# Identity products on TensorE, a weight wait split in two, and another order of the first loads in a graph layer with experts

## What is computed

```python
def graph_layer(h, adj, W_proj, b_proj, W_gcn, b_gcn):      # h = layernorm(x)
    filt = tanh(adj * adj) * (adj > 0)
    vals, idx = top_k(filt, 350)                            # per row
    new_adj = zeros_like(filt).at[rows, idx].set(vals)      # kept entries alone
    h2 = tanh(h @ W_proj + b_proj)
    return relu(new_adj @ (h2 @ W_gcn) + b_gcn)

def experts(x, Wg, bg, W1, b1, W2, b2):                     # x = layernorm(x)
    scores, idx = top_k(x @ Wg.T + bg, 2)
    probs = softmax(scores)
    return sum over e of combine[e] * (relu(x @ W1[e].T + b1[e]) @ W2[e].T + b2[e])

x = x + graph_layer(layernorm(x), adj, ...)
x = x + experts(layernorm(x), ...)
```

## Time and profile before

| | |
|---|---|
| three runs | 468.95, 470.61 and 470.99 us; median 470.61 |
| the profiled execution | 468.27 us, its span 466.5 us |
| mean granted clock of TensorE | 0.965 of the full 2.4 GHz |
| HBM | 77.9 MB read, 12.7 MB written, 194 GB/s over the span |

### The profile page before, as it was taken

One profiled execution on the slowest core, in us unless ns is written; L12 is line 12 of the kernel. 1 busy time (PEld: TensorE's weight loads), 2 busy tenths in 40 slices (PEclk: granted clock), 3 DMA queues, 4 the chain that ended last, 5 costly groups with the idle time before them and its releaser, 6 DMA issues.

```text
span 466.5 us, 8103 instructions
## 1 busy us (share of the span) xinstructions
PE 396.0 (85%) x2456; PEld 242.2 (52%) x2456; DVE 366.1 (78%) x959; ACT 339.5 (73%) x345; POOL 205.6 (44%) x266
## 2 busy tenths in 40 slices
PE   0999989999788789999998979969798989999600
PEld 0455534444334244455454434436698989989500
DVE  5999978998999999985999999999976444444235
ACT  2789998889979778859999769973565656666400
POOL 3049961000004501800740638821777777777700
PEclk9999999999999979999999999989999999999955
DMA  7839976778357666873875757854745655631069
GB/s 227 328 120 373 351 290 231 265 279 306 136 193 257 227 225 228 274 260 145 302 253 211 259 191 279 288 137 75 109 91 161 106 114 107 92 79 51 23 218 326
DMA packets 57074, 95.42 MB, mean 205 GB/s; under 512 B 36740, under 2 KB 44088, under 8 KB 48832
## 3 DMA queue, kind: packets, MB, share of 16 engines
q1 hardware_dynamic: 45840, 79.80, 52.7%
q0 software_dynamic: 6048, 12.72, 9.0%
q10 hardware_dynamic: 5136, 2.30, 1.7%
HBM read 77.90 MB, written 12.67 MB: 194 GB/s over the span
## 4 chain that ended last, share of the span: by engine, by line
DVE 50%; PE 23%; issue 12%; DMA 5%; ACT 4%; POOL 4%; ACTq 1%; SPq 1%; DVEq 0%; POOLq 0%
DVE marks L856 17%; PE bank L1350 5%; ACT tbuf L1091 3%; PE bank L1438 3%; PE bank L1458 3%; PE bank L1459 3%; PE bank L1460 2%; PE bank L1440 2%; PE bank L1439 2%; POOL expert_rows L631 2%; DMA tbuf<-expert_rows 2%; DVE rowbf L707 2%; PE bank L1297 2%; DVE tbuf L1012 2%; DVE nrm L780 1%
## 5 line engine op out<-in xcount | busy, mean ns | idle before, releaser
L1350 PE MATMUL bank<-tbuf,g_sb 128*128 128x512 f32 x512 | 236.0, 609 | 2.5 <-ACT tbuf L1095 1.6
L617 POOL DMA_INDIRECT routed_rows<-aug,slots x64 | 87.9, 1373 | 153.3 <-DVE base L834 135.6
L1350 PEld LDWEIGHTS bank<-tbuf,g_sb 128*128 128x128 f32 x512 | 95.6, 195 | 111.8 <-issue 104.7
L856 DVE SCALAR_TENSOR_TENSOR marks<-abuf,marks 128x2048 bf16<-128x2048 int32 x56 | 129.4, 2312 | 1.1
L1091 ACT ACTIVATE tbuf<-abuf 128x2048 f32<-128x2048 f32 x64 | 121.5, 1898 | 4.8 <-PE bank L1350 2.6
L1095 ACT ACTIVATE tbuf<-tbuf 128x2048 f32<-128x2048 f32 x64 | 122.3, 1911 | 2.0
L631 POOL DMA_INDIRECT expert_rows<-abuf,xmeta x78 | 76.8, 985 | 23.8 <-issue 22.0
L1012 DVE SCALAR_TENSOR_TENSOR tbuf<-bank,tbuf 128x512 f16<-128x512 f32 x78 | 50.2, 685 | 45.8 <-ACT tbuf L1198 43.0
L1458 PE MATMUL bank<-w2h,tbuf 128*128 x312 | 54.4, 219 | 2.4 <-DVE tbuf L1012 2.4
L1460 PE MATMUL bank<-w2h,tbuf 128*128 x312 | 54.3, 219 | 0.0
L1459 PE MATMUL bank<-w2l,tbuf 128*128 x312 | 54.3, 219 | 0.0
(11 more groups left out here) (216 smaller groups left out, 434.3 us busy)
## 6 DMA issues: line engine op xcount, KB each, us to landing
abuf<-in_adj_tiles SPq DMA_DIRECT2D x64, 1024.0 KB, 5.5
wstage<-in_w POOLq DMA_DIRECT2D x16, 256.0 KB, 6.5
tbuf<-expert_rows SPq DMA_DIRECT2D x8, 512.0 KB, 7.3
out<-xres ACTq DMA_DIRECT2D x8, 256.0 KB, 6.3
expert_rows<-abuf,xmeta POOLq DMA_INDIRECT x78, 2.3
routed_rows<-pad SPq DMA_DIRECT2D x9, 130.0 KB
routed_rows<-aug,slots POOLq DMA_INDIRECT x64
abuf<-routed_rows SPq DMA_TRANSPOSE x39
```

The source lines that it names most:

```text
L617: pool.indirect_dma_start(xs, bass.IndirectOffsetOnAxis(ap=slots[:, i % 2, k * SUB + cc:k * SUB + cc + 1], axis=0), aug[:, i % 2, k, cc, : ...
L856: dve.scalar_tensor_tensor(mark, bits_in, 1.0, mark, ALU.min, ALU.add).then_inc(s_raw, 1)
L1350: last = pe.matmul(ps_feat[ib % 2][:, :], g_sb[:, c, :], tbuf[:, buf, cc, :], start=(c == 0), stop=(c == C - 1))
```

## The change

- `load_x(1)` moves from ahead of chunk 0's load to behind it, and `load_x(2)` from behind chunk 0 to behind chunk 1.
- ScalarE issues W_proj first, with a semaphore of its own, `s_wp`. TensorE waits for it alone ahead of `project(0)`, and for the other three ahead of `gcn(0)`.
- ScalarE squares chunk 0 ahead of copying out group 0.
- TensorE multiplies the identity with itself 26 times (`WARM`) into bank 3 once the identity is there. The results are never read.

```diff
@@ -49,6 +49,7 @@
     NTA = NT
+    WARM = 26
     PW = 512
@@ -249,6 +250,7 @@
     s_w = sem("s_w")
+    s_wp = sem("s_wp")
@@ -406,14 +408,13 @@
             load_x(0)
-            load_x(1)
             for n in range(NCH):
                 if n >= NBUF:
                     sp.wait_ge(s_sq, n - NBUF + 1)
                     sp.wait_ge(s_raw, n - NBUF + 1)
                 sp.dma_start(abuf[:, n % NBUF, :, :], adj_tiles[n // NK, n % NK, :, :, :]).then_inc(s_a[n % NBUF], 16)
-                if n == 0:
-                    load_x(2)
+                if n < 2:
+                    load_x(n + 1)
@@ -1077,8 +1078,8 @@
+            act.dma_start(wp_sb[:, :], w_proj).then_inc(s_wp, 16)
             act.dma_start(bp_sb[:, :], b_proj.rearrange("(p o) -> p o", o=1)).then_inc(s_w, 16)
-            act.dma_start(wp_sb[:, :], w_proj).then_inc(s_w, 16)
             act.dma_start(wg_sb[:, :], w_gcn).then_inc(s_w, 16)
@@ -1111,9 +1112,9 @@
+            square_chunk(0)
             turned_out(0)
-            square_chunk(0)
-            act.wait_ge(s_w, 64)
+            act.wait_ge(s_w, 48)
             projected_out(0)
@@ -1246,6 +1247,9 @@
             pe.wait_ge(s_ident, 1)
 
+            for i in range(WARM):
+                pe.matmul(bank[3][:, 0:P], ident[:, :], ident[:, :], start=True, stop=True)
+
@@ -1269,8 +1273,9 @@
             turn_group(0)
-            pe.wait_ge(s_w, 64)
+            pe.wait_ge(s_wp, 16)
             project(0)
+            pe.wait_ge(s_w, 48)
             gcn(0)
```

## The result

In one comparison of 8 runs each, before's median was 469.81 us and the changed kernel's 472.81 us. Their ratio is 1.0087, with a 95% interval of 1.0063 to 1.0111: slower by 0.9%, or 4.1 us of 469.81. The two medians lie 3.0 us apart; of the changed kernel's eight executions five took 472.5 to 472.8 us and three 474.8 to 476.6, so that its median shows little of the spread. The predicted time, 472.8, agrees with the median largely by luck: before's median came out 0.8 us under the 470.61 that the forecast was set against, and the stall behind the loss is another than the sum's. The loss was 4.1 us where 2.2 were predicted; that is the question for the runs.

What follows compares the result with a forecast made beforehand. VectorE's chain was taken to bound the early stretch, TensorE joining at 69 us. Late x +2.2 us, other parts 0: 470.5 against the profiled 468.27, 472.8 as a median (0.47% slower); 8-in-10 range 469.4 to 475.8.

Steps and rivals of the forecast that it cites:

- The bound: VectorE's chain leads the early stretch; TensorE is on no link before 69 us, so its early gains meet none.
- It decides if chunk 1's products start before 26: Test for the rival that chunk 0's end on TensorE, not VectorE's rows, sets the pace: -3.2 us, 467.4; 8%.
- Part 1, piece 1: Load order: chunk 0 ahead of piece 1 of x lands it at 11.0 to 11.3, stalling VectorE 1.6 to 1.9 us.
- Part 1, piece 2: Load order: chunk 1 ahead of piece 2 of x lands it at 18.5, putting 2.2 us on VectorE's chain.
- Nothing absorbs it: From 28.7 to 63.5 VectorE is busy 33.7 of 34.8 us, so the 2.2 us delay carries to the end.
- Part 2: ScalarE's early square: chunk 0 lands near 10.0, group 0's copy ends 12.5, 1.2 us later than before; gain nothing.
- Part 3: TensorE's `project(0)` waits for W_proj alone: 0.6 us, off the chain and given back by the early square.
- Part 4: 26 identity products on TensorE end at 11.8, transposes 2.2 us late; 4.8 us less TensorE work, off the chain.
- TensorE didn't lead: Rival: chunk 0's end on TensorE sets the pace rather than VectorE's rows: -3.2 us, 467.4; 8%.
- x was late: Against the rival that transfers overlap and piece 2 of x lands by 16.8, VectorE unchanged: 470.6; 16%.
- the products were not too many: Against the rival that identity products stay slow, end at 15.1 and delay chunk 0 by 5.2: +4.3 us, 474.9; 7%.
- The stuck queue: Rival: piece 2 of x waits in SP's full queue and lands at 21.1: +4.8 us, 475.4; 13%.

Runs made afterwards that it cites:

- experiment 1: The changed kernel with the old load order (pieces 0 and 1 of x ahead of chunk 0, piece 2 behind it): 470.19 against 469.25 us, ratio 1.0007.
- experiment 7: The changed kernel without the 26 identity products: 473.23 us against 469.16 for the kernel before, ratio 1.0083.
- experiment 2: The kernel before with the new load order alone: 475.21 against 469.25 us, ratio 1.0132.
- experiment 8: The kernel before with POOL's first weight loads waiting for 4 normalised groups instead of 8, load 11 behind `s_const`: 467.99 against 469.16 us, ratio 0.9977.
- the first and the third of 10 to 12: The kernel before with POOL's weights earlier, split weight waits, earlier tanh, identity products; first turns group 3 behind chunk 1, third in old place: 0.9970 and 0.9953.
- experiment 4: The changed kernel with chunk 1 back behind all of x, piece 1 left behind chunk 0: 474.29 us against 469.25 for the kernel before, ratio 1.0112.
- experiment 5: The changed kernel with POOL's five small loads moved behind its first weight loads, near 33 us: 478.61 us against 469.16 for the kernel before, ratio 1.0201.
- experiment 6: The changed kernel with POOL's five small loads behind the third normalised group, about 19 us: 535.36 us against 531.83 for the kernel before, ratio 1.0058.
- experiment 3: The changed kernel with piece 1 of x back ahead of chunk 0, piece 2 behind chunk 1: 472.48 us against 469.25 for the kernel before, ratio 1.0061.
- experiment 9: The changed kernel with the old load order and 80 identity products instead of 26: 476.21 us against 469.16 for the kernel before, ratio 1.0164.
- the second kernel: The kernel before with POOL's weights earlier, split weight waits, earlier tanh, group 3 turned behind chunk 1, no identity products: 532.88 against 531.83 us, ratio 0.9988.

## Why the prediction was right or wrong

**The bound: right.** "TensorE, which the change feeds, is on no link of the chain before 69": experiments 1 and 7 give TensorE's parts a worth of nothing, and 2 gives the load order all of the loss. What the prediction underrated is how near the other path lies: in experiment 1 the chain runs through ScalarE and TensorE up to 27.8 at no cost that shows, and experiment 8 shows that about 1 us off POOL's path is enough to bring TensorE onto it for good. "It decides if chunk 1's products start before 26" is met by the first and the third of 10 to 12 (24.94 and 25.35), and both are faster than before, though by several edits at once.

**Part 1, piece 1: the step that failed.** "Piece 1: from 8.5 to 8.5 + 2.5 = 11.0, or by the other bound to where chunk 0 lands today with the same bytes ahead of and in it, 11.3." It landed at 13.7 (and the 8.5 was itself on the late side: in the seven other profiles that keep its old place piece 1 took 5.2 to 6.8 us, not 7.2), so "VectorE stalls 1.6 to 1.9 us" was 4.36 and "piece 2 decides" was false: piece 1 does, by experiment 4. Both bounds shared one mistake. They moved piece 1 by the bytes put ahead of it, at the rate of large packets, and took for granted that it meets the same engines. But the move put piece 1 into the stretch from 7 to 10 us, where before's queue had only the chunk. The prediction had the row in hand, 104 GB/s at a share of 1.13, and used it only as a chance of a gain. Read as a cost it says that some other queue holds the engines there, and POOL's was the one: 0.8 to 1.7 us by experiments 5 and 6. Some 1 us is left with those loads away (12.0 to 12.3 against 11.0 to 11.3). It isn't settled; a candidate, only argued, is x's own small packets: from 7 to 9 us SP's 783 packets carry 0.44 MB in experiment 6, some 0.56 KB each, where in before, with chunk 0 under way, 69 carry 0.46 MB.

The Trainium skill, "DMA: Bandwidth & Descriptors", section on queues, rings and completion order, says that each DMA engine takes turns between the queues it has work for, a packet at a time. By that, few slow packets on one queue delay many quick ones on another, and the rows of 7 to 9 us agree: 87 packets had 56.5% of the time.

**Part 1, piece 2: right by itself, not in the changed kernel.** "18.5 - 16.26 = 2.2 us" is 18.6 and 2.46 in experiment 3, where piece 1 keeps its place. In the changed kernel piece 2 has the same bytes ahead of it and lands at 20.2, 1.7 us later than predicted, behind a late piece 1. So the 2.2 us of the sum are no stall of the kernel that was measured, whose 4.36 us are piece 1's.

**Nothing absorbs it: right.** Marks +4.4, chunk 9 +3.9, last chunk +4.1, as "I carry 2.2 us to the end" said of its size. A part not foreseen is that a longer idle time ahead of `s_const` can let TensorE's clock fall (experiments 3 and 7: 2.12 and 2.43 us idle, then 5.38 us for 3.68), though not each time: in experiments 2 and 4 it idled 2.48 and 2.44 us and the products kept 3.68.

**Part 2: right in its worth, nothing.** Chunk 0 landed at 7.8, not 10.0. It and piece 1 have changed sides of the stretch that POOL's loads hold: it used to pass through it and now lands ahead of it. That reading is argued from the windows alone.

**Part 3: right in its worth, for another reason than given.** The wait didn't vanish, it moved. ScalarE's tanh still waits for all the weights, as its timeline shows:

```profile
12.42 0.69 ACT L1108 ACTIVATE aug<-bank,bp_sb 128x512 f32<-128x512 f32 x1 [1.74 <-DMA bg_sb<-in_b_gcn]
```

The projection ended at 11.9 and its result lay 0.5 us, until 12.42, so most of the 0.6 us won was lost again there, whatever part 2 did.

**Part 4: half right.** The products end at 9.06, well ahead of the 11.8 that I took from between the bounds and near the lower, 8.4; so the rate rose early, and the transposes were not late. (In the profiles of experiments 1, 3, 4, 5 and 6 the same products took 8.3 to 8.8 us and the transposes began at 9.7 to 10.2.) But "At the fast rate gcn takes 1.03 us less and chunk 0's products 1.75" holds for gcn and not for chunk 0 (5.80): part 1's stall opened a gap of 5.30 us in TensorE's work. I had worked out each part by itself, and the late group 1 only as a later start, at "near 17.7". It was 20.58.

**The rivals and the signs.** TensorE didn't lead, x was late, the products were not too many at 26 (experiment 9 shows the mechanism, at 80). The stuck queue didn't come: SP's long issuing, 13.07 us for two chunks from 4.25 on, lies behind piece 2, and piece 2's own took 1.06. Of the signs named for "right", x at the head of the chain and a stall for piece 1 came. The third statistics at 18 to 19 behind a wait for x (20.56, no wait), POOL's first weights near 31.3 (33.45), chunk 1's square ahead of 18.64 (21.32, behind 5.43 us of waiting for group 1) and 3.6 us for chunk 0's products (5.80) did not: all four go with the late piece 1.

## What to carry to other kernels

Order the first loads by the slack of each consumer on the path that ends last, and price a moved transfer by the queue shares of the stretch into which it falls, not by the bytes ahead of it alone; a stretch with a full share and few GB/s is a cost for whatever lands in it. Products that only keep TensorE's clock up can be worth something only when TensorE's path bounds and no long gap follows them; here both had to be arranged by other edits, which with the products gave 2.2 us. Before moving an issue "out of the way", ask what lies at its new place: the same five loads cost nothing that shows at 19 us, while at 33 us the kernel was about 5 us longer than the changed one (1.0201 against 1.0087).

## What was not expected of the hardware

POOL's small loads held 56.5% of the 16 DMA engines' time for two microseconds with 0.02 MB, 0.21 us a packet against 0.03 of SP's.

52 records of identity products took 7.46 us, an average of 0.143 us each, and up to 8.80 us in the other kernels with the same 26; at the slow rate of the earlier trace rows they would have taken 13.5, at the fast one 6.8. The granted clock in the windows stood at 1.00 all the while and up to 18 us, so ahead of its first change that column doesn't tell the level, and durations must.

In one comparison all kernels took about 62 us more, in the three that were traced there all of it behind 320 us. Nothing here tells why; the chip's number in the record, 8, is that of experiments 1 to 4, which took their usual time. One of the second kernel's twelve executions there took 1564.77 us, unexplained too.
